# A decoder layer on one core: x turned sooner, the root in step 5, waits per buffer, spread scatters, and the causal mask by 64x64 quarters

## The reference, cut to what matters

```python
# 8 sequences (batches) of 256 tokens, 128 wide
t = rmsnorm(layernorm(x)) * norm_w
q, k, v = t @ Wq, t @ Wkv[:, :1024], t @ Wkv[:, 1024:]     # 16 heads of 64
sim  = where(causal, (q @ k.T) / 8, -max);  attn = softmax(sim)
x1   = x + (sigmoid(t @ Wg) * (attn @ v)) @ Wout
x2   = x1 + retention(layernorm(x1), ctx, ctx)              # 16 heads of 8, decay mask
n3   = layernorm(x2)
top3 = top_k(n3 @ fWg, 3), softmaxed                        # 12 experts
out  = x2 + sum over top3 of w * (gelu(n3 @ Wup[e] + bup[e]) @ Wdown[e] + bdown[e])
```

## Time and profile before

| | us |
|---|---|
| median of 3 runs (lowest, highest) | 562.97 (560.76, 564.37) |
| the profiled execution | 557.62 |
| its span | 555.8 |
| PE busy | 482.0 (87%) |
| DVE busy | 393.8 (71%) |
| ACT busy | 340.4 (61%) |
| POOL busy | 281.2 (51%) |

### The profile page before, as it was taken

How to read it: one execution, slowest core, us unless ns; L and a number is a source line. 1 busy time by engine, 2 the same in 40 slices (tenths; PEclk the granted TensorE clock), 3 DMA queues, 4 the chain that set the end, 5 groups by cost and what they waited for, 6 DMA issues and landing times.

```text
span 555.8 us, 12676 instructions
## 1 busy us (share of the span) xinstructions
PE 482.0 (87%) x3683; PEld 397.1 (71%) x3683; DVE 393.8 (71%) x1324; ACT 340.4 (61%) x1012; POOL 281.2 (51%) x432
## 2 busy tenths in 40 slices
PE   2799999989998998998998999687975899999990
PEld 1567777776785885786677678456665899988880
DVE  4665668878877987887887888776983555445546
ACT  3568766766865865875776686253462666666650
POOL 3400033584375286278258447722748575565554
PEclk9989999999999999999999999778978799999996
DMA  8200000010010000000000001056554687776676
GB/s 269 83 2 1 1 2 2 1 38 0 0 33 5 0 24 14 0 14 24 0 9 29 0 0 39 1 157 174 162 111 138 184 219 214 204 190 197 186 203 153
DMA packets 58196, 42.87 MB, mean 77 GB/s; under 512 B 5059, under 2 KB 51447, under 8 KB 58160
## 3 DMA queue, kind: packets, MB, share of 16 engines
q1 hardware_dynamic: 53904, 35.42, 23.6%
q0 software_dynamic: 3824, 6.49, 3.6%
q10 hardware_dynamic: 432, 0.53, 0.4%
HBM read 31.70 MB, written 12.16 MB: 79 GB/s over the span
## 4 chain that ended last, share of the span: by engine, by line
PE 46%; DVE 19%; issue 10%; ACT 10%; another core or an unknown queue 5%; POOL 4%; SPq 3%; DMA 1%; DVEq 0%; ACTq 0%; POOLq 0%
PE zb L740 8%; PE sc L779 6%; PE ob L808 5%; PE xb L857 4%; PE xb L882 3%; PE tb_a L740 2%; PE ob L994 2%; ACT pT L613 2%; ACT p_sb L606 2%; PE tb_b L740 2%; PE tb_a L792 2%; PE tb_b L792 2%; PE sc L773 2%; PE zb L994 2%
## 5 line engine op out<-in xcount | busy, mean ns | idle before, releaser
L486 POOL TENSOR_TENSOR spare_p<-tri 128x1 f32<-128x1 f32 x94 | 26.6, 283 | 121.2 <-DVE xn L1187 67.0
L597 ACT ACTIVATE qk<-zb 128x512 f32<-128x512 f32 x64 | 38.2, 597 | 74.9 <-PE zb L740 74.9
L563 POOL DMA_INDIRECT results_by_token<-y_sb,row_i x70 | 69.9, 998 | 22.0 <-issue 19.9
L604 ACT ACTIVATE p_sb<-sc,nmx 128x128 f32<-128x128 f32 x128 | 47.0, 367 | 29.5 <-DVE nmx L1106 29.1
L779 PE MATMUL sc<-qk 64*128 64x256 f32 (+1 forms) x512 | 61.9, 362 | 0.2 <-ACT qk L597 0.2
L606 ACT ACTIVATE p_sb<-sc,nmx 128x256 f32<-128x256 f32 x128 | 61.0, 476 | 0.0
L779 PEld LDWEIGHTS sc<-qk 64*128 64x128 f32 x512 | 46.0, 194 | 16.3 <-issue 10.4
L508 POOL DMA_INDIRECT tokens_by_expert<-packed,slot_i x48 | 52.9, 1103 | 8.5 <-issue 7.5
L808 PE MATMUL ob<-pT,v_sb 128*64 128x256 f32 (+1 forms) x512 | 56.4, 342 | 0.9 <-DVE oT L1124 0.9
L1124 DVE TENSOR_TENSOR oT<-ob,pT 128x256 f32<-128x256 f32 x64 | 26.9, 420 | 36.8 <-PE ob L808 25.4
L808 PEld LDWEIGHTS ob<-pT,v_sb 128*64 128x64 f32 x512 | 31.4, 137 | 19.8 <-issue 8.8
(11 more groups left out here) (272 smaller groups left out, 1446.1 us busy)
## 6 DMA issues: line engine op xcount, KB each, us to landing
wup_sb<-in_L_ffn_Wup SPq DMA_DIRECT2D x35, 256.0 KB
wdn_sb<-in_L_ffn_Wdown SPq DMA_DIRECT2D x35, 256.0 KB
xg<-tokens_by_expert SPq DMA_DIRECT2D x35, 130.0 KB
tokens_by_expert<-padding SPq DMA_DIRECT2D x12, 260.0 KB
results_by_token<-y_sb,row_i POOLq DMA_INDIRECT x70
wkv_sb<-in_L_attn_Wkv SPq DMA_DIRECT2D x2, 512.0 KB, 6.4
ctx_b<-in_ctx SPq DMA_DIRECT2D x8, 128.0 KB
out<-x_all SPq DMA_DIRECT2D x4, 256.0 KB, 2.3
```

Source lines behind the costliest of these rows:

```text
L563: pool.indirect_dma_start(out=ys, out_offset=bass.IndirectOffsetOnAxis(ap=row_i[:, u, a:a + 1], axis=0), in_=y_sb[:, u, a, :], in_offset=None,
L597: act.activation(qk[:, :, :].rearrange("p h j -> p (h j)"), zb[:, :], ACT.Copy).then_inc(a_qk, 1)
L604: act.activation(p_sb[:, w, h, 0:P], sc[:, k, S:S + P], ACT.Exp, bias=nmx[:, w, 0, n:n + 1], accum_out=total[:, w, 0, h:h + 1])
```

## The change

- `x_T(nxt)` of step 3 stands before that step's `weigh` on PE, not behind it.
- `deviation(link, brs)` moves from the end of step 4 to the end of step 5 on DVE, and the `ratio` of pair 5, so far the first thing of step 6, stands just before it, in step 5.
- `load`: `wup` and `xg` wait for `f_row`, a new semaphore that DVE's `tokens` increments once it has copied the tile's row numbers and, newly, its weights (`weight`); `wdn` is issued last, waits for `f_dn`, and has a semaphore of its own (`ld_d`), for which `down` waits.
- On POOL the dispatch of batch 6 is written out, with the scatters of tiles 0 and 1 between its sends; the scatter loop starts at tile 2.
- The causal mask is added behind the scores by four 64x64 products on quarters of the identity, with two more mask tiles (`mask_up`, `mask_dn`) prepared by POOL at the start. Head 1's wait (`a_PA`) stands between the first two score products.

```diff
@@ load (SP)
-                    sp.wait_ge(f_y, n - DEPTH + 1)
+                    sp.wait_ge(f_row, n - DEPTH + 1)
                 ...
-                sp.dma_start(wdn_sb[:, u, :, :], ...).then_inc(ld_e[u], 16)
                 (waits for dispatched, as before)
                 sp.dma_start(xg[:, u, :, :], ...).then_inc(ld_e[u], 16)
+                if n >= DEPTH:
+                    sp.wait_ge(f_dn, n - DEPTH + 1)
+                sp.dma_start(wdn_sb[:, u, :, :], ...).then_inc(ld_d[u], 16)
@@ POOL, constants
+            pool.memset(mask_up[:, :, :], 0.0)
+            pool.memset(mask_dn[:, :, :], 0.0)
-            pool.affine_select(out=mask16[:, :, :], ..., base=0, ...).then_inc(consts, 1)
+            for m, first in ((mask_up, DH), (mask_dn, -DH), (mask16, 0)):
+                ins = pool.affine_select(out=m[:, :, :], ..., base=first, ...)
+            ins.then_inc(consts, 1)
@@ POOL, behind pack(B - 2)
-            dispatch(B - 2, pace_last)     # before send 2: queries, retained(B-1, 0); before send 5: keep
-            pack(B - 1)
-            dispatch(B - 1)
-            for n in range(TILES):         # the two scatters of tile n
+            begin(B - 2)
+            for n in range(3):
+                send(B - 2, n)
+            queries(B - 1)
+            send(B - 2, 3)
+            retained(B - 1, 0)
+            scatter(0)
+            send(B - 2, 4)
+            keep(B - 1)
+            send(B - 2, 5)
+            scatter(1)
+            pack(B - 1)
+            dispatch(B - 1)
+            for n in range(2, TILES):
+                scatter(n)
@@ scores (PE)
-                for h in range(2):
-                    if h:
-                        wait(pe, a_PA, at(b, PAIRS, s))
-                    pe.matmul(sc[:, score_bank(w, h), P:P + S]..., ident16[:, :], mask16[:, :, :], start=True, stop=False, ...)
                 pe.wait_ge(a_qk, at(b, PAIRS, s + 1))
                 for t, o, n in ((1, 0, S), (0, S, P)):
                     for h in range(2):
+                        if t and h:
+                            wait(pe, a_PA, at(b, PAIRS, s))
                         r = slice(h * DH, (h + 1) * DH)
-                        ... start=False, stop=(t == 0)
+                        ... start=(t == 1), stop=False
+                for h in range(2):
+                    for q in range(2):
+                        r = slice((q ^ h) * DH, ((q ^ h) + 1) * DH)
+                        m = (mask_up if q else mask_dn) if h else mask16
+                        ins = pe.matmul(sc[q * DH:(q + 1) * DH, score_bank(w, h), P:P + S]..., ident16[r, r], m[r, :, :],
+                                        start=False, stop=True, skip_group_check=True)
@@ step (PE)
-                if (w := lagged(cur, prev, s, 2)) ...: weigh(*w)      # now behind x_T
                 if s == 3 and nxt is not None:
                     pe.wait_ge(a_qk, at(cur, PAIRS, s + 2))
                     x_T(nxt)
+                if (w := lagged(cur, prev, s, 2)) ...: weigh(*w)
@@ down (PE)
+                pe.wait_ge(ld_d[u], (n // DEPTH + 1) * 16)
@@ step (DVE)
-                if (w := lagged(cur, prev, s, 1)) and (s != 2 if cur is not None else s < 1):
+                if (w := lagged(cur, prev, s, 1)) and (s not in (2, 6) if cur is not None else s < 1):
                     ratio(*w, link)
                 ... maxima, read_state, second_residual, scale_out, read_state
-                    if s == 4:
+                if cur is not None and s == 5:
+                    ratio(cur, 5, link)
+                if prev is not None:
+                    if s == 5:
                         deviation(link, brs)
@@ tokens, results (DVE)
                 dve.tensor_copy(row_i[:, u, :], xg[:, u, :, D].bitcast(I32))
+                dve.tensor_copy(weight[:, u, :], xg[:, u, :, D + 1]).then_inc(f_row, 1)
-                ... tensor_scalar(y_sb[:, u, a, :], y_sb[:, u, a, :], xg[:, u, a, D + 1:D + 2], None, ALU.mult)
+                ... tensor_scalar(y_sb[:, u, a, :], y_sb[:, u, a, :], weight[:, u, a:a + 1], None, ALU.mult)
```

More of the change, by code:

```diff
@@ L209, in decoder @@
         row_i = sb("row_i", [P, DEPTH, HALVES], I32)
+        weight = sb("weight", [P, DEPTH, HALVES])
         bdn_sb = sb("bdn_sb", [P, E, D])
@@ L261, in decoder @@
         ld_e = [sem(f"ld_e{u}") for u in range(DEPTH)]
+        ld_d = [sem(f"ld_d{u}") for u in range(DEPTH)]
         scattered = [sem(f"scattered{u}") for u in range(DEPTH)]
@@ L404, in _ @@
                                pattern=[[-1, P]], channel_multiplier=1).then_inc(consts, 1)
-            pool.affine_select(out=mask16[:, :, :], in_=mask16[:, :, :], compare_op=ALU.is_ge, fill=NEG, base=0,
-                               pattern=[[0, 2], [-1, P]], channel_multiplier=1).then_inc(consts, 1)
+            for m, first in ((mask_up, DH), (mask_dn, -DH), (mask16, 0)):
+                ins = pool.affine_select(out=m[:, :, :], in_=m[:, :, :], compare_op=ALU.is_ge, fill=NEG, base=first,
+                                         pattern=[[0, 2], [-1, P]], channel_multiplier=1)
+            ins.then_inc(consts, 1)
             for m in (tri, tri16):
@@ L495, in pack, with send, begin @@
                 ins.then_inc(p_pack, 1)
-            def dispatch(b, pace=None):
+            def send(b, n):
+                t, k = divmod(n, TOPK)
+                pool.indirect_dma_start(
+                    out=xs, out_offset=bass.IndirectOffsetOnAxis(ap=slot_i[:, t, k:k + 1], axis=0),
+                    in_=packed[:, t, k, :], in_offset=None).then_inc(dispatched, 16)
+            def begin(b):
                 if b == B - 1:
@@ L502, in dispatch @@
                 carry(1)
+            def dispatch(b, pace=None):
+                begin(b)
                 for n in range(T * TOPK):
@@ L769, in scores @@
                     pe.wait_ge(consts_v, 4)
-                for h in range(2):
-                    if h:
-                        wait(pe, a_PA, at(b, PAIRS, s))
-                    pe.matmul(sc[:, score_bank(w, h), P:P + S].rearrange("p (a j) -> p a j", a=2), ident16[:, :],
-                              mask16[:, :, :], start=True, stop=False, skip_group_check=True)
                 pe.wait_ge(a_qk, at(b, PAIRS, s + 1))
@@ L933, in step @@
                     logits(prev)
-                if (w := lagged(cur, prev, s, 2)) and (cur is not None or s < 2):
-                    weigh(*w)
                 if s == 3 and nxt is not None:
@@ L938, in step @@
                     x_T(nxt)
+                if (w := lagged(cur, prev, s, 2)) and (cur is not None or s < 2):
+                    weigh(*w)
                 if cur is not None:
```

29 lines of the change are left out of this document (13 added, 16 removed).

## The result

| | before | after |
|---|---|---|
| median of 4 runs each (lowest, highest) | 561.87 us (559.97, 564.37) | 567.88 us (565.78, 571.49) |
| span of the profiled execution | 555.8 us | 565.1 us |
| PE busy, DVE busy | 482.0, 393.8 us | 488.9, 396.3 us |
| mean granted clock | 0.958 | 0.959 |

The changed kernel is slower: ratio 1.013, 95% interval 1.008 to 1.018. The forecast was 558, a ratio of 0.991.

A forecast was written before the change was run, and what follows sets the result against it. PE was taken to set the loop's pace, DVE close behind. Terms -0.9 + 3.0 - 2.9 + 0.4 - 1.0 - 4.0 + 0.5 = -4.9 took the median from 563.0 to 558 us; forecast's own range 553 to 563, wider range 549 to 568.

The forecast's parts named there:

- the three copies: Chain from last projection to last plan: three DVE copies of tile weights lie in it, +0.4 us.
- the new hold: Last batch's chain: PE's completions handed on late beside the moved scatters, +0.5 us.
- The root behind the ratio: Loop, DVE: root delays the maxima of pair 6, so head 1's scores of pair 7 start 0.9 us later.
- Net of root, x and mask: +0.9 - 0.4 = +0.5 an iteration, +3.0 in six; bounds -0.3 and +1.4 each: Loop: later scores of pair 7 outweigh mask savings; x's gain is spent ahead of that wait.
- x sooner: Loop: earlier transposes free the projection of pair 5, -0.5 us an iteration; 0 if held, -1.3 if `weigh` escapes too.
- Root in the last batch: Last batch: PE's 3.7 us wait goes, about 1.2 come back ahead of pair 6's maxima, -2.5 us.
- Scatters and tokens: Experts' stage: shorter run of indirect DMAs, -4.0 us; tile 7's tokens issued ahead of `wdn`, -1.0.
- (1): Masks: the four quarters run one after another, +0.3 us a step, +14, total 572; chance 0.10.
- (2): Masks: quarter products sharing a PSUM bank wait for each other, +0.2 us a step, +9, total 567; chance 0.12.
- (3): Last batch: moved scatters delay hand-over of PE's transposes and logits by 2 to 4.5 us, total 561; chance 0.20.
- (4): Experts' stage: late hand-overs vanish, 17 tiles gain 0.4 us each, total 551; chance 0.12.
- (5): Whole kernel: no effect where PE doesn't lead; masks go two by two, late hand-overs stay, 562; chance 0.10.

The follow-up runs named there:

- mask_alone: Kernel before with only the four quarter masks placed behind the scores; ratio 1.008 (1.005 to 1.011).
- before_again: Kernel before, unchanged, profiled on the chip of the experiments; ratio 1.002 (0.999 to 1.004).
- mask_copy_later: Kernel before with the quarter masks behind the scores, and DVE's copy of `region` moved behind the first norm's root; ratio 1.004 (1.002 to 1.006).
- x_alone: Kernel before with only the next x turned ahead of `weigh`; ratio 1.001 (0.998 to 1.004).
- root_last_batch: Kernel before with the root moved to step 5 in the last batch only, loop untouched; ratio 1.000 (0.994 to 1.006).
- scatters_alone: Kernel before with only the scatters of tiles 0 and 1 spread among the dispatch; ratio 0.999 (0.997 to 1.002).
- after_root_back: Changed kernel with the root back in step 4 ahead of pair 4's ratio, pair 5's ratio again in step 6; ratio to before 1.010 (1.007 to 1.014).
- changed_root_in_halves: Changed kernel with the root taken back to step 4 and cut in two halves; ratio to before 1.008 (1.004 to 1.012).
- root_alone: Kernel before with only the root's move behind the ratio of pair 5; ratio 1.023 (1.020 to 1.026).
- changed_again: Changed kernel, unchanged, run beside the kernel before on the chip of the experiments; ratio 1.028 (1.023 to 1.032).

## Why the prediction was wrong

Forecast -4.9 us, measured +9.3 by the two spans. The 14.2 us between them: the six periods 6.2 (+3.0 forecast, +9.2 measured), the start 2.5 (-0.9, +1.6), from the last x to tile 0 3.5 (-2.0 with the three copies and the new hold, +1.5), the tiles 0.5 and the end 1.5.

- **The root behind the ratio: mechanism and size right.** Maxima of pair 6 forecast 0.9 us late, 1.1 measured; the wait ahead of head 1's scores of pair 7 was named. At full clock the period grew by 1.1.
- **The step that failed is "Net of root, x and mask: +0.9 - 0.4 = +0.5 an iteration, +3.0 in six; bounds -0.3 and +1.4 each".** Two terms in it. The masks' -0.3 to -0.5 an iteration are -0.03 (44.27 in mask_alone, 44.30 in before_again, means of the last four). And the price of a 2-us wait was taken as its length, with nothing for the clock: the mean is +1.5 (270.8 - 261.6 over six), outside the bounds. The falls of the clock behind it, 1.3 to 1.5 us in three of the periods, are 4.3 of these 9.2 us; without them it would be +0.8, inside the bounds. I looked at the clock of the stretch as it was ("granted in full") and never asked what the new wait would do to it.
- **Why the masks give nothing.** Each undisturbed step is 0.09 us shorter, in batch 0 too (3.67 for 3.76). But the mask used to run in places where it was cheap: under the wait for ACT's copy of q and k (in steps 0, 1 and 2 the scores now take 0.91 to 1.00 us, not 0.85), and between products: x's transposes grow from 0.27 to 0.37 and the last counts' product from 0.12 to 0.23 us, now that scores follow them. Behind that stands DVE, 36.9 us busy of 44, which paces steps 4 to 6.
- **"The two extra memsets and selects on POOL lie beside the first loads: 0"** was wrong by 1.2 us, and is shown (10.4 to 9.2 in mask_copy_later), though 0.5 to 0.7 us of it are left at later marks. I named no work that hides them.
- **x sooner: right as forecast.** The projection was freed, `weigh` stayed held, and part of the gain was spent in a wait for the retention product (0.62 us). x_alone is worth nothing on a chip without holds, where there is nothing to win; on one with them it wasn't run alone.
- **Root in the last batch: -2.5, with the masks -2.9; measured -1.6 at most.** The wait went and two came. From pair 3's scores to tile 0 after takes 35.5 us for 37.1 before; root_last_batch gained 0.4 there against before_again, and its ratio is 1.000. Ahead of these scores, in the rest of batch 6, after lost 3.1 us, where its pair 7 has the loop's wait once more: hence +1.5 from the last x to tile 0.
- **Scatters and tokens: -5.0, measured -4.6** (tiles 0 to 7 +1.2, 7 to 8 -5.8). The scatters' mechanism is as told; the tokens' term isn't: tile 7 waits 1.77 us for its tokens, not 2.27, so 0.5 of the 1.0 came, and tile 7 comes no sooner after the last batch (1.2 us later behind tile 0), which the prediction had named as a sign of being wrong. DVE's longest wait is 5.5 us, not under 3. The forecast didn't ask whether that hold is a property of the kernel: on four of the chips it hardly shows, and the term is 0.
- **Not forecast at all:** +1.5 us in the end, where ACT and DVE are held once more on the last tiles; every kernel on a chip without holds has 20.6 to 20.7 us there. The phase of a hold is not a thing that I could have read.
- **The rivals.** (1) and (2) fell: four products in 0.23 us, two of them in each bank from different rows. The rule of the Trainium skill, "TensorEngine Tiling (Array Packing)", section Restrictions and Gotchas, that such products can't use a bank at the same time, doesn't show in the time here: these rows start within 0.01 us. (3) isn't shown: tiles 0 to 7 take 0.7 us more in scatters_alone and 1.2 in after, but 1.3 and 2.7 more in x_alone and mask_alone, which move no scatter. (4) fell: 98.2 for 98.1. (5) came true by another way, for the masks alone. None of them had a fall of the clock, though (3) set a wait in place of another.
- **A reading.** The first 32.26 us of the tiles' stage hold nine tiles, 3.58 us each on the mean and not 3.44: the first two take 4.17 and 4.07, the others 3.43 to 3.47. The sum doesn't use it.

**Open.** mask_alone less its start is still 0.4% slower than before. The traces put it into the last batch and the first tiles, where the share of time at half clock differs from kernel to kernel: a mean clock of 0.964 (mask_copy_later) against 0.981 (before_again) is 39 against 20 us at 1.2 GHz. Runs of one kernel go the same way: of the 19 of before beside mask_copy_later the five with a mean clock of 0.978 or more took 536.2 to 538.0 us, the two with 0.963 or less 540.1 and 541.5. That these falls are the cause is argued, not shown; a filler in one place moved the fall to another. What the hold is, and why two of the six chips seen show it, wasn't found; nor were fewer or wider-spaced indirect DMAs in the loop tried against it. Nor was after_root_back run on a chip with holds; the nearest to it there, changed_root_in_halves, has a wait of 2 us at another place, so the root's old place isn't shown to mend the change on such a chip.

## What to carry to other kernels

A wait on PE has two prices, its length and what the clock does behind it. Before moving work behind the last idle stretch, compare the new wait with the longest that the loop has had at full clock; here waits of 1.5 us did no harm and most of those of 2.1 did. A chain of tiny dependent instructions can be cut and put into more than one idle stretch; here that gained what fitted into the stretch, 0.45 of 1.2 us, and nothing on a chip whose idle stretch lay elsewhere. Work added to a set-up needs a look at who waits for the end of that set-up. And a loss that shows as a late hand-over should be looked for on a second chip before a change is built on it.

## What the runs showed of the hardware

- The same kernel takes 538 to 563 us by chip. Span 555.8 and 534.5: six periods to x of batch 7 261.6 and 259.7, tiles 7 to 8 9.6 and 3.8, 8 to 34 98.1 and 89.7, the end 22.1 and 20.7.
- The clock fell behind PE's idle stretches of 2.1 to 2.5 us in most iterations (three of five in after, four in root_alone and changed_again, the fourth each time without, though the stretch was as long) and behind none of 1.5 us in the loop. Sixteen unused products in the wait stopped it.
- Four 64x64 bf16 products of 256 columns, one on each quarter of the array and two in each PSUM bank, start within 0.01 us of each other and take 0.22 to 0.23 us together.
